# Hybrid block: expert routing of batches 0 to 6 woven into the softmax stage, batch 7 routed in the expert stage

## The reference

```python
# attention b, on the layer norm of x
qkv = batch @ (sigma_param / sigma * W_qkv)        # 16 heads of 8, causal softmax, then @ W_proj
x = x + attention_b(_layernorm(x))
# mixture of experts, on the layer norm of x: Wr (128, 8), W1 (8, 128, 512), W2 (8, 512, 128)
x = x + experts(_layernorm(x), Wr, W1, W2)         # top 2 of 8 by x @ Wr, softmax over the two, relu between W1 and W2
```

## Time and profile before

| | us |
|---|---|
| median of 3 executions | 1838.96 |
| lowest and highest | 1828.43, 1912.0 |
| the profiled execution | 1830.69 |
| its span, first to last instruction | 1828.9 |
| PE busy over the span | 1316.1 (72%) |
| DVE busy | 1071.5 (59%) |
| POOL busy | 834.1 (46%) |
| ACT busy | 774.4 (42%) |

### The profile page before, as it was taken

The page is one execution under the profiler, slowest core; times in us unless marked ns, Lnnn a source line. Parts: engine busy times, 40 slices in busy tenths (PEclk is TensorE's granted clock), DMA queues, the critical chain, the costliest instruction groups (busy, mean ns, idle before and its releaser), DMA issues. The chain is left out here.

```text
span 1828.9 us, 36163 instructions
## 1 busy us (share of the span) xinstructions
PE 1316.1 (72%) x11164; PEld 849.2 (46%) x11165; DVE 1071.5 (59%) x3170; ACT 774.4 (42%) x1286; POOL 834.1 (46%) x1221
## 2 busy tenths in 40 slices
PE   5763259963988888832299817888899995957486
PEld 3542159961233333322299812333345554734364
DVE  2654425445877877444255456767576634749765
ACT  1221113211466666711033204776655555735274
POOL 2116745533233333357555536766654413447252
PEclk9985579985799999955599956998999998978698
DMA  3004122245323222041122230000000000000001
GB/s 104 0 16 122 42 63 69 67 118 128 71 80 85 66 65 65 3 126 41 58 68 68 59 95 1 1 2 1 2 2 2 1 2 1 1 1 1 1 1 47
DMA packets 87712, 79.80 MB, mean 44 GB/s; under 512 B 11791, under 2 KB 77583, under 8 KB 87280
## 3 DMA queue, kind: packets, MB, share of 16 engines
q1 hardware_dynamic: 76898, 57.16, 12.1%
q0 software_dynamic: 8704, 17.97, 2.9%
q10 hardware_dynamic: 1980, 3.00, 0.8%
HBM read 46.07 MB, written 32.01 MB: 43 GB/s over the span
## 5 line engine op out<-in xcount | busy, mean ns | idle before, releaser
L1146 ACT ACTIVATE grp_pt<-ps 128x1024 f32<-128x1024 f32 (+2 forms) x320 | 244.7, 799 | 212.2 <-PE ps L1223 133.9
L2035 DVE TENSOR_REDUCE soft_mx<-ps 128x2 f32<-128x1024 f32 (+3 forms) x256 | 201.9, 821 | 57.0 <-PE ps L1873 55.7
L680 POOL DMA_INDIRECT products<-moe_product,moe_rows_in x144 | 152.9, 1062 | 151.9 <-DVE moe_product L852 142.3
L1759 ACT ACTIVATE soft_pt<-ps 128x768 f32<-128x768 f32 (+1 forms) x192 | 166.3, 884 | 83.2 <-PE ps L1904 81.6
L707 ACT ACTIVATE moe_hid<-ps 128x512 f32<-128x512 f32 x144 | 85.8, 597 | 249.9 <-PE ps L744 234.2
L1680 POOL TENSOR_SCALAR_AFFINE_SELECT soft_pt<-soft_pt 128x256 f32<-128x256 f32 (+1 forms) x192 | 92.7, 483 | 208.9 <-ACT soft_pt L1759 208.4
L744 PE MATMUL ps<-moe_rT,moe_W_now 128*128 128x128 f32 x1152 | 157.2, 280 | 2.0 <-issue 2.0
L1243 PE MATMUL ps<-grp_pt,grp_vpad 128*32 128x160 f32 (+4 forms) x2048 | 145.6, 393 | 15.9 <-POOL grp_pt L1088 15.7
L753 PE MATMUL ps<-moe_W,moe_hid 128*128 x1152 | 155.2, 278 | 1.3 <-ACT moe_hid L707 1.1
L658 POOL DMA_INDIRECT sorted_rows<-moe_row,moe_target x128 | 124.8, 975 | 50.2 <-issue 35.7
L744 PEld LDWEIGHTS ps<-moe_rT,moe_W_now 128*128 128x128 f32 x1152 | 143.2, 196 | 5.5 <-issue 5.4
(11 more groups left out here) (335 smaller groups left out, 2754.2 us busy)
## 6 DMA issues: line engine op xcount, KB each, us to landing
moe_rows_in<-sorted_rows SPq DMA_DIRECT2D x144, 65.0 KB, 1.8
moe_back<-products SPq DMA_DIRECT2D x16, 512.0 KB, 7.2
soft_kst<-soft_scratch_k SPq DMA_DIRECT2D x32, 192.0 KB
moe_W<-in_W SPq DMA_DIRECT2D x2, 2048.0 KB, 8.5
moe_W<-in_W SPq DMA_DIRECT2D x16, 256.0 KB, 6.9
soft_scratch_q<-soft_parts SPq DMA_DIRECT2D x16, 192.0 KB, 2.7
soft_qst<-soft_scratch_q SPq DMA_DIRECT2D x32, 96.0 KB
soft_scratch_k<-soft_parts SPq DMA_DIRECT2D x14, 192.0 KB, 2.8
```

Source lines behind the costliest of these rows:

```text
L680: pool.indirect_dma_start(k.products, bass.IndirectOffsetOnAxis(rows_in[:, u, DEST_COL:DEST_COL + 1].bitcast(U32), 0), product[:, u, :], N ...
L1146: act.activation(at.pair(pt[:, s % 2, :], pair, seg)[:, :, 0:w], ring[(chunks_before(m) + c) % 2][:, :, 0:w], ACT.Exp, scale=scale).then_i ...
L1759: act.activation(LATENT.pair(pt[:, s % 2, :], pair, seg)[:, :, 0:w], ring[second_turn(n, c) % RING3][:, :, 0:w], ACT.Exp, scale=scale).the ...
L2035: ins = dve.tensor_reduce(mx[:, tile, half, :, r], ring[first_turn(n, d) % RING3][:, :, at:at + keys], AX.X, ALU.max)
```

## The change

The routing's helpers become a class `Routing` with its own tiles and semaphores, in a stage "route" that encloses the softmax stage and the second expert stage. The routing of batch m (0 to 6) is written into the positions of the softmax stage: the statistics at position 19 of batch m+1, powers at 20, the normalizing on ACT (in place of DVE) and the second copy of the rows at 22, the transposes at 23, the product with Wr at position 1 of batch m+2, the choice at 2 to 7, the ranks at 15, and the eight scatters at positions 18, 20, 22 and then 0, 2, 4, 6, 8. The transpose, copy and spread of the maxima's second half move by one position. What is left of batches 5 and 6 is issued behind the last position. The second expert stage (`experts_routed`) routes batch 7 alone, then makes the table, the fills and the expert steps as before. The first expert stage stays as it was.

```diff
+class Routing:
+    def gone(self, eng, m):
+        if m >= 0:
+            eng.wait_ge(self.scattered[m % 2].sem, self.scattered[m % 2].at(m // 2))
+    def apply(self, act, m):
+        act.wait_ge(self.powered.sem, self.powered.at(m))
+        self.gone(act, m - 2)
+        for j in range(T):
+            ins = act.activation(self.row[:, m % 2, j, 0, 0:P], self.k.x[:, m * T + j, :], ACT.Identity, bias=self.shift[:, j:j + 1],
+                                 scale=self.rstd[:, j:j + 1])
+        ins.then_inc(self.normed.sem, 1)
+    def turn(self, pe, m, bank):
+        pe.wait_ge(self.normed.sem, self.normed.at(m))
+        for j in range(T):
+            ins = pe.transpose(bank[:, j * P:(j + 1) * P], self.row[:, m % 2, j, 0, 0:P], self.k.ident)
...
+    def scatter(self, pool, m, i):
+        j, s = divmod(i, 2)
+        if i == 0:
+            pool.wait_ge(self.dest_set.sem, self.dest_set.at(m))
+            pool.wait_ge(self.steps.sem, self.steps.at(m, self.TARGET))
+        pool.indirect_dma_start(self.k.sorted_rows, bass.IndirectOffsetOnAxis(self.target[:, m % 2, s, j:j + 1], 0),
+                                self.row[:, m % 2, j, s, :], None).then_inc(self.scattered[m % 2].sem, 16)
...
             for n in range(B):
                 for c in range(PASS):
                     keep(n, c)
+                    if n > 2 and c < 10 and c % 2 == 0:
+                        route.scatter(pool, n - 3, 3 + c // 2)
+                    if n > 1 and c == 16:
+                        route.number(pool, n - 2)
+                    if n > 1 and c in (18, 20, 22):
+                        route.scatter(pool, n - 2, (c - 18) // 2)
+                    if n > 0 and c == 20:
+                        route.power(pool, n - 1)
...
+            for i in range(3, 2 * T):
+                route.scatter(pool, B - 3, i)
+            route.number(pool, B - 2)
+            for i in range(2 * T):
+                route.scatter(pool, B - 2, i)
...
-                    if c == 2:
+                    if c == 3:
                         copy_maxima(n, 1)
...
-                    if c == 4:
+                    if c == 5:
                         spread_maxima(n, 1)
+                    if c == 5 and n > 1:
+                        route.exponent(act, n - 2)
...
+                    if c == 22 and n > 0:
+                        route.apply(act, n - 1)
+                        route.repeat(act, n - 1)
+                    if c == 23 and n > 0:
+                        route.copy_xT(act, n - 1, bank[HALF_B])
...
+                    if n > 1:
+                        pe.wait_ge(route.steps.sem, route.steps.at(n - 2, route.LOGIT))
...
+                        if half == 1 and n > 1:
+                            pe.wait_ge(route.steps.sem, route.steps.at(n - 2, route.PLACED))
...
+                    if c == 15 and n > 1:
+                        if n + 1 < B:
+                            pe.wait_ge(m_copied.sem, m_copied.at(n + 1, 1))
+                        else:
+                            pe.wait_ge(aT_ready.sem, aT_ready.at(n - 1))
+                        route.rank(pe, n - 2, bank[HALF_A])
...
-                    if c == 2:
+                    if c == 1 and n > 1:
+                        route.gate(pe, n - 2, bank[HALF_B])
+                    if c == 3:
                         turn_maxima(n, 1)
...
+                    if n > 1:
+                        if c == 2:
+                            route.read_logits(dve, n - 2, bank[HALF_B])
+                        if c == 4:
+                            route.choose(dve, n - 2)
+                        if c == 7:
+                            route.gates(dve, n - 2)
+                        if c == 15:
+                            route.aim(dve, n - 2, bank[HALF_A])
                     if c == 18 and n > 0:
                         add(n - 1)
+                    if c == 19 and n > 0:
+                        dve.wait_ge(added.sem, added.at(n - 1))
+                        route.stats(dve, n - 1)
                     if c == 20:
                         divide(n, 0)
```

More of the change, by code:

```diff
@@ L1507, in _, with soft_attention @@
             add(UNITS2 - 1)
-def soft_attention(nc, k):
+def soft_attention(nc, k, route):
     PAIRS2 = H // 2
@@ L1697, in _ @@
             power(3)
+            route.prepare(pool)
             for n in range(B):
@@ L1817, in _ @@
                         copy_v(n + 1)
+                    if c == 22 and n > 0:
[3 more added lines that the diff above has]
+                        route.copy_xT(act, n - 1, bank[HALF_B])
             drain(B - 1, 1)
+            route.exponent(act, B - 2)
             copy_aT(B - 1)
@@ L1994, in _ @@
                         project_v(n + 1)
+                    if c == 23 and n > 0:
+                        if n + 1 < B:
+                            pe.wait_ge(v_copied.sem, v_copied.at(n + 1))
+                        else:
+                            pe.wait_ge(divided.sem, divided.at(n, 2))
+                        route.turn(pe, n - 1, bank[HALF_B])
             for c in range(LAG):
                 values_at(B, c)
+                if c == 1:
+                    route.gate(pe, B - 2, bank[HALF_B])
             turn_sums(B - 1, 1)
+            pe.wait_ge(exp_done.sem, exp_done.at(B - 1))
+            route.rank(pe, B - 2, bank[0])
             turn_back(B - 1)
@@ L2779, in hybrid_kernel @@
         if "soft" in todo:
-            soft_attention(nc, k)
-        if "moe2" in todo:
-            experts(nc, k, io, "moe2")
+            with Stage(nc, "route") as st:
+                st.ctx.callback(st.clear)
+                route = Routing(st, k)
+                soft_attention(nc, k, route)
+                experts_routed(nc, k, io, "moe2", route)
         if "grouped" in todo:
```

347 lines of the change are left out of this document (added).

## The result

The changed kernel took 1788.02 us (median of four runs, 1785.97 to 1791.25), the kernel before 1835.26 beside it: a ratio of 0.9755, with a 95% interval of 0.9721 to 0.9789. It is faster by 2.5%; 1785 was predicted. The profiled execution of the changed kernel took 1788.7, 42.0 us less than that of before.

A forecast was written before the change was run, and what follows sets the result against it. POOL's scatters were taken to pace the routing, PE's list the softmax stage. 1828.9 - 87.4 + 25.5 + 3.1 + 12.2 + 1.0 = 1783.3 us span, with 1.8 around it 1785; likeliest case 1775 to 1796, 2 in 10 outside 1764 to 1812.

The forecast's parts named there:

- The expert stage: Second expert stage routes only batch 7: 26.4 us to the first fetch instead of 113.8, gain 87.4 us.
- Rival 5: Expert stage's fetch held by fills behind the load of W or late landings of batch 6: +10 to +15, 1798; chance 0.05.
- The loop, 28.6 with batch 7: Softmax stage: routing work and waits added in batches 0 to 6, 25.5 us, plus 3.1 in the last batch.
- The wait for the counts: Values at position 16 wait for DVE's `placed` behind a 1.2 us maximum: 0.5 us in five batches, 2.5.
- Laid out by hand this exponent ends 1.5 us later: 0.6 of it PE's own work, 0.9 a new wait: The turn (row transposes at position 23) delays exponent 23: over six batches 3.6 us of work plus 5.4 of waits.
- The reorder: Maxima's copy moved from position 2 to 3: PE's 0.89 us wait shrinks by about 0.5, -1.5 in all.
- The statistics: DVE at position 19, 1.3 us into 0.71 idle: division and value projection 0.65 late, six batches, 3.9 us.
- The choice: DVE at position 4: second projection 0.4 us late in batches 4 and 5, 1.75 in 2 and 3; 4.3 in all.
- rival 2: In the softmax stage new waits fall where PE would have waited anyway; only its work is paid: 1765, chance 0.15.
- Scatters in the loop at nothing: POOL's 43 loop scatters cost nothing in batches 2 to 6, covered by about 4 us slack before PE uses a keep.
- The tail, 12.2: Softmax stage's end: POOL's remaining scatters of batches 5 and 6 end it 12.2 us later, behind the last batch's 3.1.
- The gap, 1.0: Between softmax and second expert stage: one more barrier and the outer stage's clearing add 1.0 us to 3.4.

The follow-up runs named there:

- after_again: The changed kernel, unedited, measured once more on another chip: 1782.73 us, ratio 0.9711 to the kernel before.
- place_first: Changed kernel with DVE adding ranks to places ahead of its maximum at position 15; ran once, windows 2 and 4 to 6 changed by -0.62 to -0.63 us.
- doubled: Changed kernel with each of the 43 scatters inside the softmax loop issued twice, the second to a tensor nothing reads: 1810.94 us, ratio 0.9866.
- late_all: Changed kernel with batch 6's number columns and all eight scatters issued in the second expert stage, not at the softmax stage's end: 1784.58 us, ratio 0.9733.
- tail_reordered: Changed kernel with batch 6's eight scatters, gates and targets in the expert stage and its product with Wr, choice and ranks later in the tail: 1771.46 us, ratio 0.9656.
- stats_later: Changed kernel with the routing's statistics behind the division at position 20 and POOL's powers behind keep 21; ran once, about +0.4 us in each window.
- late_four: Changed kernel with only the last four of batch 6's eight scatters moved into the second expert stage: 1784.84 us in its one run.

## Why the prediction was right, step by step

*The total* was right within 3 us of the median and 4 of the profiled execution (span 1786.9 for 1783.3), in part by luck, because misses cancel: 7.5 us too much on the loop with batch 7 and 0.8 on the expert stage; 4.8 too little on the tail and 3.6 on the gap. What is left over, 3.5, is the start of the stages, the first batches and the drift of untouched code. The softmax stage as a whole grew by 38.5 us, where the sum's terms make 40.8, inside the prediction's own limits of 25 and 60.

*The expert stage: right.* 26.4 us to the first fetch were predicted, 25.6 measured (88.2 gained for 87.4). The fills ended beside the scatters as forecast: issued by 849.41, the last scatter began at 850.15 and ended at 851.10, and the fetch came 3.4 us behind its start, as counted. The way to the first scatter took 12.7 us for 14.15, the seven further ones 9.5 for 8.8 (one of them took 1.50). Rival 5 is out.

*The loop, 28.6 with batch 7: mechanism right, waits mis-sized.* Windows 2 to 7 grew by 21.1 us, 19.8 in after_again. PE's added work was right: 1.7 to 1.9 us a batch for 1.9, where the clock stayed up. The wait for the counts was right, 0.55 for 0.5, and place_first took it away. Four terms were off. The step "Laid out by hand this exponent ends 1.5 us later: 0.6 of it PE's own work, 0.9 a new wait" failed: PE waits 0.65 for the scaled rows, but then 0.4 less for the exponent, so some 0.25 is new where 0.9 was counted; 4 of the 5.4 us weren't there. The reorder was worth 0.74 a batch and not 0.5, except in windows 2 to 4, where the read of the logits takes it back, as the prediction said. The statistics cost 0.4 a batch, not 0.65. The choice cost nothing in window 5 (0.4 counted) and less than its 1.75 in 2 and 3: these are 1.5 and 2.0 longer than window 5 in after_again. In window 3 0.83 of that is the read of the logits, the rest PE's waits for `rest_part` (1.0 for 0.5) and a maximum (0.6). So rival 2 was partly right, for the turn alone.

*Batch 7: nearly right.* Its window grew by 3.5 to 3.7 us where 3.1, and 2.15 for the turn and the statistics, were counted; the 1.6 too many are mostly these two, mis-sized as above.

*Scatters in the loop at nothing: right,* shown by the second set of doubled (0.14 us each). The cover named, 4 us ahead of a keep's use, wasn't the tightest; the power steps' was.

*The tail, 12.2: 3 to 5 too low.* It grew by 17.0 us, 15.2 in after_again. From the targets to the last scatter's end it took 10.6 us for 10.2; the miss lies ahead of that. "Last exponent 2.6 late" failed: POOL's powers kept ACT waiting 2.1 us, the last keep came 4.6 late, and then the product with Wr stood ahead of the last values, with PE at a granted clock of 0.67 over the tail (0.86 before), which no term of the sum held.

```profile
796.17 1.65 ACT L948 ACTIVATE route_row<-x,route_shift,route_rstd 128x128 f32<-128x128 f32 x4 [2.11 <-POOL route_shift L942]
...
800.41 1.88 PE L971 MATMUL ps<-pack,route_xT 128*128 128x8 f32 x8
...
805.65 0.60 ACT L2197 ACTIVATE soft_summed<-ps 128x512 f32<-128x512 f32 x1 [5.97 <-remote]
```

The last row holds the other 1.9 us: ACT's copy of the sums waited that much longer than in after_again (4.12), with PE's values done at the same distance. The trace names no engine for it, and it is left open.

*The gap, 1.0: wrong, 4.6.* "One more barrier and the clearing of the outer stage" looked at clears. The outer stage's clear costs 0.2 (the gap behind the expert stage is 3.39 for 3.15). What lay on the path is POOL's DRAIN, 4.64 us behind the last scatter. None of the rows taken from before shows it, but that trace has one, 6.59 us long, at the end of each expert stage, hidden. Its rate, 0.082 us for each scatter, came out in the later runs alone. late_all shows it by its absence.

*The clock:* 1.00 in the loop as forecast, but for the dip in one window; 0.67 in the tail.

## What to carry to other kernels

Work woven into a loop that one engine paces costs about its own instructions on that engine; a new wait just ahead of an old one can take its place in good part (0.65 new took 0.4 off the next here), so price the sum of the two afterwards, not the new one alone. The expensive part of such a change is its end: what the woven work leaves behind the last iteration stands uncovered, and GpSimd's DRAIN ends later by 0.08 us for each indirect DMA of the stage, wherever it stood (4.6 us for 56 here; with 136 it was 6.6). If it can't be fewer of them, let the last be over well before the other engines are done: here, with eight of them in the next stage, the gap fell from 8.0 to 3.4 us, and the first fetch came 1.4 us later (tail_reordered).

Read the clock of each window before an edit is charged with a difference: a dip is worth as much as the waits sought here.

## What the hardware did that was not expected

- GpSimd's DRAIN at the end of a stage takes 0.082 to 0.083 us for each indirect DMA that the stage issued, 48 to 99 of them: it ended 3.98 to 4.64 us behind the last in eleven profiles, and 8.15 where the loop's scatters were doubled. With 136 it took 6.59, no more than with 80. In the changed kernel the bytes had stopped moving 3.4 us before its end. What it does in that time isn't shown.
- The same program repeats its windows 2 and 4 to 6 to 0.02 us (window 7 to 0.23), apart from single events: a dip of PE's clock to 0.96 in window 3 (1.06 us, in six of the twelve profiles of kernels with the change; in stats_later it lies in windows 5 and 6, in doubled a second one in window 7), and a pause of 1.9 us in the tail (in the changed kernel, late_all and late_four). A difference of 1 or 2 us between two profiles can be such an event; the window in which it lies tells.
- SP's eight fills took 15.4 us in late_all and 8.1 to 9.2 in the eleven other profiles.
